# An attention kernel's last quad: a smaller early softmax, plain order at the end, earlier lookups, and repeated matmuls on TensorE

## The reference

```python
emb = jax.vmap(lambda tbl, idx: tbl[idx], in_axes=(0, 1), out_axes=1)(embed_tables, sparse)
bi = emb[:, FIRST, :] * emb[:, SECOND, :]                 # 325 pairs of 26 fields
a = relu(einsum('bpd,dh->bph', bi, att_w_w) + att_w_b)    # 32 -> 8
scores = einsum('bph,ho->bpo', a, att_d_w) + att_d_b
att_out = sum(softmax(scores, axis=1) * bi, axis=1)
out = sigmoid(concatenate([att_out, dense], -1) @ fin_w + fin_b)
```

## Time and profile before

| | |
|---|---|
| median of 3 executions | 479.94 us (479.78 to 482.1) |
| profiled execution | 481.23 us, of which the span from first to last instruction is 479.4 us |
| busy share | DVE 83%, PE 78%, POOL 70%, ACT 39% |
| mean granted TensorE clock | 0.896 |

### The profile page before, as it was taken

One profiled execution on the slowest core, in us unless ns is written; L12 is line 12 of the kernel. 1 busy time (PEld: TensorE's weight loads), 2 busy tenths in 40 slices (PEclk: granted clock), 3 DMA queues, 4 the chain that ended last, 5 costly groups with the idle time before them and its releaser, 6 DMA issues.

```text
span 479.4 us, 9758 instructions
## 1 busy us (share of the span) xinstructions
PE 375.4 (78%) x2676; PEld 214.9 (45%) x2676; DVE 399.4 (83%) x638; ACT 185.2 (39%) x414; POOL 334.3 (70%) x350
## 2 busy tenths in 40 slices
PE   1596687978689698879789797978789698876753
PEld 1585554534228565535138564534228565511110
DVE  5999797897876999997857998897876999998723
ACT  3203313353453223454363222453453223465362
POOL 5777777777777777777777777777777777777000
PEclk9888979998799899998799899998799899987576
DMA  8467323222223333132223323242213232222000
GB/s 289 76 151 154 24 16 25 16 25 15 17 13 25 25 16 25 16 26 14 17 14 25 26 14 26 16 24 15 15 15 15 14 15 13 15 15 13 4 0 1
DMA packets 16310, 15.35 MB, mean 32 GB/s; under 512 B 7952, under 2 KB 15488, under 8 KB 15872
## 3 DMA queue, kind: packets, MB, share of 16 engines
q0 software_dynamic: 11072, 5.69, 23.2%
q1 hardware_dynamic: 2800, 6.79, 4.0%
q10 hardware_dynamic: 2384, 2.25, 1.7%
HBM read 14.68 MB, written 0.02 MB: 31 GB/s over the span
## 4 chain that ended last, share of the span: by engine, by line
DVE 32%; PE 25%; POOL 17%; issue 14%; ACT 7%; DMA 3%; another core or an unknown queue 1%; DVEq 0%; POOLq 0%; ACTq 0%
POOL emb L416 17%; DVE ring L831 14%; PE first L463 10%; PE sums L480 8%; DVE onehot L731 7%; PE looked L446 5%; DVE look_masked L816 4%; ACT hidden L557 3%; DMA emb<-tables,rows 2%; ACT shared L588 2%; DVE emb_t L807 2%; DVE emb L819 1%; DVE shared L845 1%; PE sums L488 1%
## 5 line engine op out<-in xcount | busy, mean ns | idle before, releaser
L416 POOL DMA_INDIRECT emb<-tables,rows x300 | 284.8, 949 | 91.5 <-issue 89.7
L446 PE MATMUL looked<-look_parts,onehot 128*128 128x448 f32 x896 | 207.9, 389 | 25.1 <-DVE onehot L731 16.6
L446 PEld LDWEIGHTS looked<-look_parts,onehot 128*128 128x128 f32 x896 | 175.6, 201 | 74.1 <-issue 35.9
L831 DVE TENSOR_TENSOR ring<-emb_t,turned 128x512 f32<-128x512 f32 (+9 forms) x180 | 191.8, 1100 | 0.3
L557 ACT ACTIVATE hidden<-first,par 128x512 f32<-128x512 f32 x168 | 104.7, 674 | 155.2 <-PE first L463 154.6
L463 PE MATMUL first<-ring,weights 64*32 64x512 f32 (+1 forms) x1344 | 101.6, 663 | 56.2 <-DVE ring L831 40.2
L807 DVE STREAM_TRANSPOSE emb_t<-emb 128x128 f32<-128x128 f32 x100 | 29.8, 303 | 46.0 <-ACT turned L625 33.9
L480 PE MATMUL sums<-hidden,par 128*32 128x512 f32 (+1 forms) x336 | 58.8, 733 | 7.1 <-ACT hidden L557 7.1
L731 DVE TENSOR_TENSOR onehot<-chunk_of,turned 128x896 fp32r<-128x896 f16 x60 | 63.2, 1053 | 0.0
L463 PEld LDWEIGHTS first<-ring,weights 64*32 64x32 f32 x1344 | 16.6, 109 | 102.5 <-DVE ring L831 73.3
L625 ACT ACTIVATE turned<-emb_t 128x128 f32<-128x128 f32 x92 | 25.9, 282 | 87.5 <-DVE emb_t L807 81.0
(11 more groups left out here) (66 smaller groups left out, 86.6 us busy)
## 6 DMA issues: line engine op xcount, KB each, us to landing
emb_placed<-tables SPq DMA_DIRECT2D x768, 0.1 KB
emb<-tables,rows POOLq DMA_INDIRECT x300, 3.5
ring<-tables SPq DMA_DIRECT2D x1, 1568.0 KB, 10.5
hidden<-tables SPq DMA_DIRECT2D x1, 1568.0 KB, 9.7
shared<-tables SPq DMA_DIRECT2D x1, 1568.0 KB, 8.5
chunk_of<-chunk_numbers ACTq DMA_DIRECT2D x12, 128.0 KB, 3.3
hidden<-tables SPq DMA_DIRECT2D x1, 896.0 KB, 5.6
emb<-tables,rows_first POOLq DMA_INDIRECT x44, 4.0
```

Of the source, the lines that this page charges most:

```text
L416: pool.indirect_dma_start(emb[:, f, g * D:(g + 1) * D], None, stacked, bass.IndirectOffsetOnAxis(ap=row, axis=0), element_offset=at,).then ...
L446: mm = nc.tensor.matmul(looked_rows[tile % 2], onehot[:, tile % ONEHOTS, c, :], look_parts[:, n, c, k, :], start=c == 0 and k == 0, stop=c ...
L831: nc.vector.tensor_tensor(slot[:, at:at + n, :], emb_t[:, i:i + n, :], turned[f % 2][:, 0, :].unsqueeze(1).broadcast_to((P, n, P)), ALU.mu ...
```

## The change

The early softmax covers three batches (groups 0 to 11, 192 pairs) and the late one 133 pairs. In every quad the early maximum stands at field 23 on DVE and the early exponentials at field 24 on ACT. The eager order of the last quad is gone: all quads use the same order. The rows of field 24 are put in place at field 21. The last quad's twelve lookups stand at fields 1 to 12, one to a field. And in the last quad, at each of fields 15 to 25, PE repeats the 14 matmuls of the last lookup into a PSUM bank that nothing reads any more, ahead of the field's first group.

```diff
-SP_PLACE = 23
+SP_PLACE = 21
 TILE_FIELDS = (1, 2, 4, 5, 6, 8, 9, 10, 11, 13, 14, 16, 18, 20, 22)
+TILE_FIELDS_LAST = tuple(range(1, 13))
+BUSY_FIELDS = range(15, 26)
-        fields = TILE_FIELDS + (F,)
+        fields = TILE_FIELDS + (F,) if q < QUADS - 1 else TILE_FIELDS_LAST
-    EARLY = BATCHES - 2
+    EARLY = BATCHES - 3
# PE
+                def keep_busy(f):
+                    if q == QUADS - 1 and f in BUSY_FIELDS:
+                        pe.wait_ge(look_masked_done, TILES)
+                        for c in range(CHUNKS):
+                            for k in range(PARTS):
+                                nc.tensor.matmul(looked_rows[0], onehot[:, (TILES - 1) % ONEHOTS, c, :],
+                                                 look_parts[:, LOOKS - 1, c, k, :], start=True, stop=True)
                         if gr == done[-1]:
                             beside(f)
+                        if gr == done[0]:
+                            keep_busy(f)
                         first_products(gr)
-                        if gr - 1 in batch_ends[:EARLY] and not ends_early(q, gr - 1):
+                        if gr - 1 in batch_ends[:BATCHES - 2]:
                             score_products(batch_ends.index(gr - 1))
-                        if gr - 2 in batch_ends[:EARLY] and not ends_early(q, gr - 2):
+                        if gr - 2 in batch_ends[:BATCHES - 2]:
                             turn_back(batch_ends.index(gr - 2))
-                        if ends_early(q, gr):
-                            score_products(EARLY - 1)
-                            turn_back(EARLY - 1)
+                keep_busy(F - 1)
                 for gr in groups_of(F - 1):
-                    if last and gr == GROUPS - 3:
-                        score_products(BATCHES - 2)
-                        turn_back(BATCHES - 2)
                     first_products(gr)
-                    if not last and gr == GROUPS - 3:
+                    if gr == GROUPS - 3:
                         score_products(BATCHES - 2)
-                    if not last and gr == GROUPS - 2:
+                    if gr == GROUPS - 2:
                         turn_back(BATCHES - 2)
# ACT: copy_second and homes follow the same order; and
-                    if q == QUADS - 1 and f == EARLY_FIELD:
-                        copy_second(BATCHES - 2)
-                        homes(BATCHES - 2)
+                    if f == EARLY_FIELD:
                         exponentiate_early()
                 copy_second(BATCHES - 1)
-                if q < QUADS - 1:
-                    exponentiate_early()
-                else:
+                if q == QUADS - 1:
                     finals_end_home(q)
                     exponentiate_late(q)
# DVE
-                    if q == QUADS - 1 and f == EARLY_FIELD:
+                    if f == EARLY_FIELD - 1:
                         early_maximum()
                 if q < QUADS - 1:
-                    early_maximum()
                     make_onehot(end_tile, 0)
```

More of the change, by code:

```diff
@@ L76, in attention_fm @@
     TILES = QUADS * TILES_Q
-    assert len(TILE_FIELDS) + 1 == TILES_Q and CHUNK_BLOCKS == LOOKS
+    assert len(TILE_FIELDS) + 1 == TILES_Q and len(TILE_FIELDS_LAST) == TILES_Q - G and CHUNK_BLOCKS == LOOKS
     def place_of(tile):
@@ L87, in tiles_beside @@
         at = G + q * TILES_Q
-        fields = TILE_FIELDS + (F,)
+        fields = TILE_FIELDS + (F,) if q < QUADS - 1 else TILE_FIELDS_LAST
         return [at + k for k, beside in enumerate(fields) if beside == f and at + k < TILES]
     for q in range(QUADS):
-        for f in TILE_FIELDS:
+        for f in range(1, F):
             for tile in tiles_beside(q, f):
@@ L146, in batches_through_group @@
         return 1 + sum(1 for end in batch_ends if end < gr)
-    EARLY_FIELD = 1 + next(f for f in range(F) if EARLY_GROUPS in groups_of(f))
-    assert EARLY_FIELD == F - 2
+    EARLY_FIELD = F - 2
     def pairs_c(gr):
@@ L340, in chunk_numbers_of @@
             return rows.broadcast_to((P, n * G * P))
-        def ends_early(q, gr):
-            return q == QUADS - 1 and gr == EARLY_GROUPS - 1
         block = ctx.enter_context(nc.Block())
@@ L499, in _ @@
                             beside(f)
+                        if gr == done[0]:
+                            keep_busy(f)
                         first_products(gr)
-                        if gr - 1 in batch_ends[:EARLY] and not ends_early(q, gr - 1):
+                        if gr - 1 in batch_ends[:BATCHES - 2]:
                             score_products(batch_ends.index(gr - 1))
-                        if gr - 2 in batch_ends[:EARLY] and not ends_early(q, gr - 2):
+                        if gr - 2 in batch_ends[:BATCHES - 2]:
                             turn_back(batch_ends.index(gr - 2))
-                        if ends_early(q, gr):
-                            score_products(EARLY - 1)
-                            turn_back(EARLY - 1)
                     if not done:
                         beside(f)
-                last = q == QUADS - 1
+                keep_busy(F - 1)
                 for gr in groups_of(F - 1):
-                    if last and gr == GROUPS - 3:
+                    first_products(gr)
+                    if gr == GROUPS - 3:
                         score_products(BATCHES - 2)
-                        turn_back(BATCHES - 2)
-                    first_products(gr)
-                    if not last and gr == GROUPS - 3:
-                        score_products(BATCHES - 2)
-                    if not last and gr == GROUPS - 2:
+                    if gr == GROUPS - 2:
                         turn_back(BATCHES - 2)
@@ L646, in _ @@
                         relu_group(gr)
-                        if gr - 1 in batch_ends[:EARLY] and not ends_early(q, gr - 1):
+                        if gr - 1 in batch_ends[:BATCHES - 2]:
                             copy_second(batch_ends.index(gr - 1))
-                        if gr - 2 in batch_ends[:EARLY] and not ends_early(q, gr - 2):
+                        if gr - 2 in batch_ends[:BATCHES - 2]:
                             homes(batch_ends.index(gr - 2))
[L651 to L654, removed]
+                        if gr == GROUPS - 3:
                             copy_second(BATCHES - 2)
-                        if q < QUADS - 1 and gr == GROUPS - 2:
+                        if gr == GROUPS - 2:
                             homes(BATCHES - 2)
-                    if q == QUADS - 1 and f == EARLY_FIELD:
-                        copy_second(BATCHES - 2)
-                        homes(BATCHES - 2)
+                    if f == EARLY_FIELD:
                         exponentiate_early()
                 copy_second(BATCHES - 1)
-                if q < QUADS - 1:
-                    exponentiate_early()
-                else:
+                if q == QUADS - 1:
                     finals_end_home(q)
```

## The result

The changed kernel takes 486.76 us (median of 4 executions, 485.99 to 487.78); the old one, measured beside it, 480.96. The ratio is 1.0122, with a 95% interval of 1.0083 to 1.0162: slower, by 5.8 us or 1.2%. The forecast was 487.3. The profiled execution took 487.39 us, with a span of 485.6; the sum had given 486.8 for the span.

What follows compares the result with a forecast made beforehand. Gathers were taken to bound the last quad, then a half-clock tail; with repeats, PE. From 412.4, 62.3 us of PE work and waits, 4.2 to the last turn's end and 7.9 behind gave span 486.8, median 487.3, range 478 to 491.

Steps and rivals of the forecast that it cites:

- the sum: PE's work and waits in the last quad from 412.4 on, through the tail: span 486.8, 7.4 us more than 479.4.
- The step on which the sign hung: Last quad, PE's queue: eleven repeats of 3.04 us, 33.4 us, delay every field because matmuls stay in program order.
- The first repeat: Last quad on PE: starts at 412.4, after group 5 and the turning back of batch 0.
- group 5: Last quad: its pairs complete at 410.7, from 408.7 plus 3.5 takes, plus 0.5 maximum, minus 2.0 earlier DVE entry.
- The stalls between groups: PE waits for relus where two groups follow with no repeat between: 1.4, 1.4 and 0.8, together 3.6 us.
- a turn ahead of a repeat: PE's turning back of a score batch in the last quad, counted at 0.66 us each, 2.6 for four.
- The end behind it: From the last turn to the end of the span: 6.8 us before, 7.9 with the larger late softmax.
- PE's room: Old kernel, 412.4 to 472.6: 29 us of waits or half clock, of which the repeats want 33.4.
- the no-change rival: PE just has room for the repeats: all three lower bounds together, -7.4 us, give 479.9; chance 0.12.
- the slow clock of the tail: Last quad's tail: PE at half clock, 0.50 at 450 to 455; a score batch takes 3.63 against 1.92.
- the order at the end: Last quad's end: same groups, batches and copies issued in another order; effect taken as contained in the sum.
- the first rival: Last quad: repeats hidden, clock stays up, DVE decides; span 467.5, 11.9 less, median 468; chance 0.14.

Runs made afterwards that it cites:

- the curve of lengths: Changed kernel with 0, 7, 10 or 14 matmuls in each repeat, against the old kernel: 469.98, 470.02, 476.38 and 486.76 us.
- the plain order: Old kernel with only the eager order at the end of the last quad taken out: 473.81 us, ratio 0.9856.

## Why the prediction was right, and where its reasons were not

*What decides.* The step on which the sign hung, that eleven repeats fill PE and that nothing can pass them, is shown: by the trace, in which every group of the changed kernel starts when the repeat ahead of it ends, and by the curve of lengths. The Trainium skill (TensorE: Matmul & The Clock Gate, Step-by-step: what each phase is for) has matmuls stay in program order; the trace agrees: DVE's first piece of field 15, begun at 413.31 and about 1 us long, completed group 6, and the group was started at 416.42, when the repeat had ended.

*The terms.* The first repeat was put at 412.4 and began at 413.40. DVE entered the quad 2.1 us earlier (361.88 against 363.98), as taken; the 1.3 by which group 5 then was late (411.96 against 410.7) I had not counted. DVE waits there for PE's lookups at fields 1 and 2 (0.66 and 0.30 in the list of its idle times), and whether that is all of it was not tried. A repeat was put at 3.04 and took 3.02, a group 1.02 and took 1.02, a batch 1.86 and took 1.86. The stalls between groups were put at 3.6 and came to 0.94 + 0.94 + 0.35 = 2.2; a turn ahead of a repeat was put at 0.66 and cost 0.41 (as at 412.99 to 413.40), three times behind the first repeat. Together: +1.0 - 1.4 - 0.75 = -1.15, and the last turn ended at 477.74 in place of 478.9. The end behind it was put at 7.9 us and took 7.86. That the forecast of 487.3 lies only 0.5 from the median is in part luck: errors of both signs cancel, and the profiled execution, which I had put 1.3 above the median, stood 0.6 above it.

*The bounds.* PE's room was put at 29 us of waits and half clock, of which the repeats would want 33.4. The lengths show it smaller, close to 17.7; that fits with the 11 us by which the rest of the change shortened the kernel. By the working of the no-change rival, everything would have had to go PE's way by 7.4 us; it did by 1.2.

*What was wrong.* I read the tail as held by the half clock: "the change has something to win, the slow clock of the tail". The half clock is there, but what it holds is small. In the new order it costs up to about 1.7 us by the estimate above, and repeats that lift it take as much: with and without them the order ends at 469.1 and 468.5, or 467.7 and 467.8. In the old order some 2.2 us of the half clock lie open behind group 20, and the plain order wins them without repeats. And I said of the order at the end only that its effect is in the sum; it is the largest gain in the change, some 7 us with the clock that comes with it, before the 4 us of the early softmax. So the first rival had the right price, 467.5, for another reason than I gave: take out the repeats, and the order and the smaller early softmax bring it to within 1 us (468.5), with the clock at half in fields 23 and 24. The forecast came out because its sum followed PE's queue in the new order, and did not ask what held the old one.

*Not on the path:* the lookups at fields 1 to 12 and the placing at field 21, as taken (0 in the sum but for the start of the repeats).

## What to carry to other kernels

Work that is put on an engine to keep its clock up has to be counted in that engine's queue like any other: here about 17.7 us of it went into waits and into what the faster clock gave back, and the rest was paid in full, one for one. Before paying for a clock, take the filler out and look whether the time changes at the lower clock, and look in the chain that ended last for what the slow stretch costs: here it was some 2 us, in part by an estimate, and filler that stands in the same chain ate that up. And an order that finishes a batch early is only good if nothing that ends the kernel stands behind it on the same engine.

## What the runs showed of the hardware that was not expected

The granted clock is not fixed by the program alone. Between 415 and 425 the runs without repeats and with repeats at the last three fields are the same program on every engine up to field 22; the windows of the first, then of the second:

```profile
415.00:420.00 5.00, 2.88 (x36) 0.67 0.21 11
420.00:425.00 5.00, 4.97 (x36) 0.65 0.28 13
```

```profile
415.00:420.00 5.00, 3.02 (x43) 1.00 0.20 12
420.00:425.00 5.00, 3.72 (x48) 1.00 0.26 13
```

In the first PE had stood idle for 2.12 us ahead of 417.67, and the next group took 1.96; in the second its gap there was 1.36, and the group took 1.09. DVE had waited 0.67 us for a gather in the first just before. The length of that one gap does not tell the two apart: the run with short repeats at fields 20 to 24, up to there the same program too, has the slow group behind a gap of 1.36.

```profile
416.74 1.96 PE L470 MATMUL first<-ring,weights 64*32 64x512 f32 x16 [1.36 <-ACT hidden L560]
```

What tips the clock was not tried. It cost the first run nothing that its end shows: DVE still waited 0.77 us for field 23's gather, up to 437.80.
